# First attention layer of a two-layer kernel: mixes together behind the scores, a score bank for two of eight turns, layer norm's last step on GpSimd

## The reference, cut to what matters

```python
x = x + L0(_gn(x), ...)      # x: 1 x 128 rows x 256 tokens x 256 channels
x = x + L1(_gn(x), ...)      # _gn: group norm over all rows and tokens, 32 groups

def L0(x1d, x2d, ...):       # 8 heads of 32
    x = layernorm(x1d) * norm_w + norm_b
    q, k, v = split(x @ qkv_w.T)
    gate = sigmoid(x @ gate_w.T + gate_b)
    bias = x2d @ x2d_w.T / sqrt(32)              # the same for all 128 rows
    weights = softmax(q k^T + bias, over keys)    # 256 x 256, per row and head
    return ((weights v) * gate) @ final_w.T + final_b

def L1(x, ...):              # 4 heads of 64, keys within 16 of the query
    return banded_attention(x @ w_in.T + b_in) @ w_out.T + b_out
```

## Time and profile before

| | us |
|---|---|
| median of 3 runs (lowest, highest) | 3706.16 (3704.67, 3711.67) |
| the profiled execution, and its span | 3711.91, 3710.0 |
| busy PE, DVE, ACT, POOL over the span | 3428.1, 3129.4, 2693.5, 1993.3 |
| layer 0: first and last `ln_rstd` | 218.5, 2345.7 |
| between the layers: aggregation starts | 2398.8 |
| granted TensorE clock, mean | 0.973 of full speed |

### The profile page before, as it was taken

The page is one execution under the profiler, slowest core; times in us unless marked ns, Lnnn a source line. Parts: engine busy times, 40 slices in busy tenths (PEclk is TensorE's granted clock), DMA queues, the critical chain, the costliest instruction groups (busy, mean ns, idle before and its releaser), DMA issues.

```text
span 3710.0 us, 122532 instructions
## 1 busy us (share of the span) xinstructions
PE 3428.1 (92%) x36747; PEld 2986.1 (80%) x36747; DVE 3129.4 (84%) x11359; ACT 2693.5 (73%) x8871; POOL 1993.3 (54%) x3723
## 2 busy tenths in 40 slices
PE   4469999999999999999999999799999999999998
PEld 1157878777878787878787787599999999999998
DVE  4479999999999999999999999778888888888887
ACT  1148888888888888888888888567677667766776
POOL 0046767666666666666666666434434344444443
PEclk8579999999999999999999999899999999999999
DMA  9921111111111111111111111111111111111111
GB/s 360 354 71 46 49 46 48 48 45 50 43 51 42 51 42 51 42 51 42 51 42 51 42 51 42 41 41 51 51 56 51 51 51 57 51 51 52 55 51 47
DMA packets 189032, 238.42 MB, mean 64 GB/s; under 512 B 11824, under 2 KB 176176, under 8 KB 184752
## 3 DMA queue, kind: packets, MB, share of 16 engines
q1 hardware_dynamic: 184368, 204.17, 17.4%
q10 hardware_dynamic: 4608, 33.56, 2.5%
HBM read 170.57 MB, written 67.11 MB: 64 GB/s over the span
## 4 chain that ended last, share of the span: by engine, by line
PE 49%; DVE 16%; issue 13%; POOL 11%; ACT 5%; DMA 4%; DVEq 1%; ACTq 0%; POOLq 0%; SPq 0%
PE work L464 20%; POOL prob L359 6%; PE score L597 5%; PE work L473 5%; PE turn L504 5%; PE mix L630 4%; ACT prob L702 4%; PE score L491 3%; DMA x_chunk<-xT 3%; PE turn L614 3%; POOL g_tok L373 2%; POOL g_tok L370 2%; DVE kT L954 2%; DVE att L939 2%; DVE y_sb L890 2%
## 5 line engine op out<-in xcount | busy, mean ns | idle before, releaser
L359 POOL TENSOR_SCALAR prob<-prob,row_inv 128x256 f32<-128x256 f32 x2048 | 1049.0, 530 | 683.3 <-DVE row_inv L908 670.7
L464 PE MATMUL work<-src,w 128*128 128x256 f32 x7680 | 1074.1, 289 | 36.4 <-DVE y_sb L890 29.9
L702 ACT ACTIVATE prob<-prob,row_min 128x256 f32<-128x256 f32 x2048 | 1022.6, 504 | 39.2 <-DVE row_min L902 39.2
L464 PEld LDWEIGHTS work<-src,w 128*128 128x128 f32 x7680 | 951.9, 189 | 118.9 <-DVE y_sb L890 59.7
L902 DVE CUSTOM_DVE_ANT_0 prob<-score,neg_bias 128x256 f32<-128x256 f32 x2048 | 753.1, 419 | 111.7 <-PE score L491 100.9
L402 POOL TENSOR_SCALAR prob<-prob,row_inv 128x160 f32<-128x160 f32 x1024 | 387.9, 397 | 765.0 <-DVE row_inv L1012 765.0
L504 PE MATMUL turn<-ident,prob 128*128 128x128 f32 x4096 | 627.9, 276 | 35.2 <-DVE probT L913 29.7
L708 ACT COPY probT<-turn 128x512 f32<-128x512 f32 x512 | 299.5, 585 | 351.4 <-PE turn L504 351.4
L765 ACT ACTIVATE prob<-prob,row_min 128x160 f32<-128x160 f32 x1024 | 431.1, 426 | 136.4 <-DVE row_min L1005 136.3
L504 PEld LDWEIGHTS turn<-ident,prob 128*128 128x128 f32 x4096 | 463.9, 141 | 78.8 <-POOL prob L359 47.0
L464 PE MATMUL work<-att,wf 128*128 128x256 f32 x3072 | 429.3, 289 | 3.6 <-DVE att L939 2.2
(11 more groups left out here) (99 smaller groups left out, 5528.2 us busy)
## 6 DMA issues: line engine op xcount, KB each, us to landing
pair_chunk<-pairT ACTq DMA_DIRECT2D x32, 1024.0 KB, 7.7
x_chunk<-xT SPq DMA_DIRECT2D x32, 1024.0 KB, 8.4
x_sb<-xT SPq DMA_DIRECT2D x128, 256.0 KB, 3.4
x_tok<-x_nat SPq DMA_DIRECT2D x128, 256.0 KB, 3.3
x1T<-y_sb SPq DMA_DIRECT2D x128, 256.0 KB, 2.2
x_sb<-x1T SPq DMA_DIRECT2D x128, 256.0 KB, 2.9
outT<-y_sb SPq DMA_DIRECT2D x128, 256.0 KB, 2.2
prob<-w_d SPq DMA_DIRECT2D x1, 1024.0 KB, 8.2
```

Source lines behind the costliest of these rows:

```text
L359: pool.tensor_scalar(prob[:, h, ib], prob[:, h, ib], row_inv[:, h, ib:ib + 1], 1.0, ALU.mult, ALU.mult).then_inc(norm_done[0], 1)
L464: ins = pe.matmul(out[:, cb], w[:, of_w, kb, cols + cb * P:cols + (cb + 1) * P], x[:, of_x, kb], start=n == 0, stop=n == len(terms) - 1)
L702: act.activation(prob[:, h, ib], prob[:, h, ib], ACT.Exp, bias=row_min[:, h, ib:ib + 1], scale=-1.0, accum_out=row_sum[:, h, ib:ib + 1]).t ...
```

## The change

Seven things change in layer 0. (1) `mixes(last, 0)` and `mixes(last, 1)` stand together behind `scores(m, 1)`; before, half 0 stood in the row's own body. (2) Heads 3 and 7 are transposed into the first score bank, not into `turn`; VectorE copies them from there, and each half's scores wait for the copy. (3) The banks of the projections are dealt anew: q, k and gate in bank 0; transposed `xn`, v and y in bank 1. (4) GpSimd computes `xn` as g * rstd + off, with off = -mean * rstd from a small product of its own, one row further ahead. (5) ScalarE, not VectorE, copies the rounded part of `src`. (6) The residual leaves `final_b` out and is one addition over 512 columns, at the start of a later body; `final_b` enters layer 1's statistics as an offset and its output through `y_bias`. (7) The output statistics are taken for two rows at once, so half as many are aggregated. The order of the bodies changes on every engine. Layer 1's loop keeps its order.

```diff
 # GpSimd, body0: ahead = m + 3
+                if far.exists:
+                    wait(pool, ln_var_done, far.times(2, 2))
+                    apart(pool, pool_passed)
+                    pool.tensor_tensor(ln_rstd[:], ln_var[:], minus_half[:], ALU.pow).then_inc(ln_rstd_done, 1)
+                    wait(pool, ln_rstd_done, far.times(2, 1))
+                    pool.tensor_tensor(ln_off[:], ln_neg[:], ln_rstd[:], ALU.mult).then_inc(ln_rstd_done, 1)
+                    wait(pool, ln_rstd_done, far.times(2, 2))
+                    wait(pool, t2_done, far.times(1, 0))
+                    apart(pool, pool_passed)
+                    for tb in range(TB):
+                        pool.tensor_scalar(xn[:, tb], g_tok[:, far.base % 2, tb], ln_rstd[:, tb:tb + 1],
+                                           ln_off[:, tb:tb + 1], ALU.mult, ALU.add).then_inc(xn_done, 1)
...
 # TensorE, body0
                 def scores(r, hg):
...
+                    wait(pe, turn_done[0][1], r.times(PAIRS0, 2 * hg - 2))
...
                 def turns(h):
                     wait(pe, norm_done[0], m.times(TB * H0, TB * (h + 1)))
-
-                    if h % 2 == 0:
+                    to = turn[:]
+                    if h % HPG == HPG - 1:
+
+                        to = score[:, 0].rearrange("p b t -> p (b t)")
+                        if h < HPG:
+                            wait(pe, min_done[0], m.times(TB * H0, TB * (HPG + 1)))
+                        elif nxt.exists:
+                            wait(pe, min_done[0], nxt.times(TB * H0, TB))
+                    elif h % HPG == 0:
+                        wait(pe, turn_done[0][0], m.times(PAIRS0, h // 2))
+                    elif h % HPG == 1:
+                        wait(pe, turn_done[0][0], m.times(PAIRS0, h // 2 + 1))
+                    else:
                         wait(pe, turn_done[0][1], m.times(PAIRS0, h // 2))
...
+                if nxt.exists:
+                    wait(pe, src_done[0], nxt.times(1, 1))
+                    wait(pe, gate_done, m.times(HG, HG))
+                    project(work[:, 0], w0, 0, x).then_inc(q_ps[0], 1)
                 if m.exists:
                     scores(m, 1)
+                if last.exists:
+                    mixes(last, 0)
+                    mixes(last, 1)
+                if m.exists:
                     turns(0)
...
                 if m.exists:
                     turns(2)
-                if nxt.exists:
-                    wait(pe, q_done[0], nxt.times(1, 1))
-                    project_tokens(work[:, 0], w0, 2 * CH, x).then_inc(v_ps[0], 1)
-                if m.exists:
                     turns(3)
                 if nxt.exists:
+                    if far.exists:
+                        wait(pe, xnT_done, far.times(CB, CB))
+                    else:
+                        wait(pe, y_done[0], m.times(1, -1))
+                    project_tokens(work[:, 1], w0, 2 * CH, x).then_inc(v_ps[0], 1)
                     scores(nxt, 0)
                 if m.exists:
                     turns(4)
+                if nxt.exists:
+                    wait(pe, k_done[0], nxt.times(1, 1))
+                    project(work[:, 0], w0, 3 * CH, x).then_inc(gate_ps, 1)
+                if m.exists:
+                    turns(5)
...
 # ScalarE, body0
+                    wait(act, xnT_done, far.times(CB, CB))
+                    wait(act, gate_ps, far.times(1, -1))
+                    act.copy(src[:, far.base % 2, HIGH], xnT[:]).then_inc(src_high[0], 1)
...
 # VectorE, body0 (done = m - 2)
+                    dve.tensor_tensor(y_sb[:, :, done.base % 2], work[:, 1], x_sb[:, done.base % XSLOTS], ALU.add
+                                      ).then_inc(y_done[0], 1)
...
-                if far.exists:
-                    wait(dve, ln_rstd_done, far.times(1, 1))
-                    wait(dve, t2_done, far.times(1, 0))
-                    for tb in range(TB):
-                        dve.tensor_scalar(xn[:, tb], g_tok[:, far.base % 2, tb], ln_mv[:, tb, 0:1],
-                                          ln_rstd[:, tb:tb + 1], ALU.subtract, ALU.mult).then_inc(xn_done, 1)
...
+                    dve.tensor_scalar(ln_neg[:], ln_mv[:, :, 0], -1.0, None, ALU.mult).then_inc(ln_var_done, 1)
                     dve.tensor_scalar(ln_var[:], ln_mv[:, :, 1], EPS, None, ALU.add).then_inc(ln_var_done, 1)
...
+                if done.exists and done.base % 2 == 1:
+                    wait(dve, y_done[0], done.times(1, 1))
+                    apart(dve, dve_passed)
                     for ob in range(CB):
...
+                        dve.bn_stats(gstat1[:, ob, at], y_sb[:, ob].rearrange("p r t -> p (r t)")).then_inc(y_stats, 1)
```

More of the change, by code:

```diff
@@ L351, in body0, with norms @@
             def body0(m):
-                nxt, far = m + 1, m + 2
-                def norms(r, g):
-                    wait(pool, inv_done[0], r.times(PAIRS0, g + 1))
+                nxt, far, ahead = m + 1, m + 2, m + 3
+                g = g_tok[:, ahead.base % 2]
+                def norms(r, j):
+                    wait(pool, inv_done[0], r.times(PAIRS0, j + 1))
                     apart(pool, pool_passed)
-                    for h in (2 * g, 2 * g + 1):
+                    for h in (2 * j, 2 * j + 1):
                         for ib in range(TB):
@@ L716, in body0 @@
                     act.copy(nqT[:, nxt.base % 2, HIGH], work[:, 0]).then_inc(q_high[0], 1)
+                if m.exists:
+                    exps(m, 3)
+                    exps(m, 4)
+                    turn_copy(0)
+                if far.exists:
+                    wait(act, t2_done, far.times(1, 1))
+                    wait(act, src_done[0], far.times(1, 0))
+                    for cb in range(CB):
+                        act.activation(xnT[:, cb], work[:, 1, cb], ACT.Identity,
+                                       scale=vec0_sb[:, 0, cb:cb + 1], bias=vec0_sb[:, 1, cb:cb + 1]
+                                       ).then_inc(xnT_done, 1)
+                    wait(act, xnT_done, far.times(CB, CB))
+                    wait(act, gate_ps, far.times(1, -1))
+                    act.copy(src[:, far.base % 2, HIGH], xnT[:]).then_inc(src_high[0], 1)
+                if m.exists:
+                    exps(m, 5)
+                if nxt.exists:
+                    wait(act, k_ps[0], nxt.times(1, 1))
+                    act.copy(kT[:, nxt.base % 2, HIGH], work[:, 0]).then_inc(k_high[0], 1)
+                if m.exists:
+                    turn_copy(2)
                 if last.exists:
@@ L747, in body0 @@
                 if nxt.exists:
-                    exps(nxt, 3)
-                    wait(act, gate_ps, nxt.times(1, 1))
-                    wait(act, att_sum_done, nxt.times(1, -1))
-                    for hg in range(HG):
-                        act.activation(gate[:, nxt.base % 2, hg], work[:, 1, hg], ACT.Tanh, scale=0.5,
-                                       bias=half_gate_b[:, hg:hg + 1]).then_inc(gate_done, 1)
+                    exps(nxt, 2)
             over_rows(act, 2, 1, body0)
@@ L880, in split @@
                                   ).then_inc(src_done[n], 1)
-            def residual(n, last, bank, bias):
-                wait(dve, y_ps[n], last.times(1, 1))
-                wait(dve, y_out[n][last.base % 2], last.times(16, 0, of=2))
-                if n == 0:
-                    wait(dve, x_in[n][last.base % XSLOTS], last.times(16, 16, of=XSLOTS))
-                    apart(dve, dve_passed)
-                for ob in range(CB):
-                    dve.scalar_tensor_tensor(out=y_sb[:, last.base % 2, ob], in0=work[:, bank, ob], scalar=bias[:, ob:ob + 1],
-                                             in1=x_sb[:, last.base % XSLOTS, ob], op0=ALU.add, op1=ALU.add
-                                             ).then_inc(y_done[n], 1)
             def body0(m):
-                last, nxt, far = m + -1, m + 1, m + 2
+                last, nxt, far, ahead = m + -1, m + 1, m + 2, m + 3
                 def mins(r, h):
@@ L940, in body0 @@
                                       ).then_inc(att_done[0], 1)
-                if far.exists:
-                    wait(dve, g_done[0], far.times(1, 1))
+                if nxt.exists:
+                    mins(nxt, 0)
+                if m.exists:
+                    inverse(m, 3)
+                if nxt.exists:
+                    mins(nxt, 1)
+                    mins(nxt, 2)
+                if m.exists:
+                    turn_copy(5, turn[:])
+                if nxt.exists:
+                    mins(nxt, 3)
@@ L1026, in body1 @@
                 if (last + -1).exists:
-                    residual(1, last + -1, 1, vec1_sb[:, 2])
+                    done = last + -1
+                    wait(dve, y_ps[1], done.times(1, 1))
+                    wait(dve, y_out[1][done.base % 2], done.times(16, 0, of=2))
+                    for ob in range(CB):
+                        dve.scalar_tensor_tensor(out=y_sb[:, ob, done.base % 2], in0=work[:, 1, ob],
```

(2 more changed lines are left out.)

238 lines of the change are left out of this document (107 added, 131 removed).

## The result

| | before | after |
|---|---|---|
| median of 4 runs each, same chip (lowest, highest) | 3708.90 (3704.67, 3711.67) | 3661.44 us (3654.74, 3664.15) |
| ratio, 95% interval | | 0.987, 0.9852 to 0.9888 |
| profiled execution, span | 3711.91, 3710.0 | 3664.15, 3662.3 |
| layer 0's row, from the power step | 16.75 | (2292.4 - 223.4) / 127 = 16.29 |

What follows compares the result with a forecast made beforehand. PE's own work was the floor: 15.32 of layer 0's 16.75 us row. Waits of 0.58 and 0.02 made 15.92, plus 0.05 and 0.08, 16.05: 89 us less, seams -1, so 3616 us; range 3560 to 3725, the forecast's own 3590 to 3648.

Steps and rivals of the forecast that it cites:

- The wait ahead of head 1: On PE, head 1's turn awaits head 0's copy out of the one `turn` bank: 0.58 us in every row.
- The two paths: Through PE's order and through ScalarE's and VectorE's copies, the next row's scores were to be reached within 0.02 us.
- the mixes' lead-in: PE's delay before mixes behind scores, taken as 0.17 us; other values would shift the row by -0.17 to +0.09.
- there the layout leaves no slack, and I add 0.05: Every second row, VectorE's double statistics precede the residual, q's remainder and head 4's minima: 0.05 us added.
- rival C: Slower: delays in the loop through ScalarE to the next scores are paid in full; 17.05 us a row, 3743 us; chance 0.19.
- ScalarE's copy of head 0 starts at s+3.65: Start of ScalarE's string to the next scores, 3.65 us after `scores(m, 1)` starts on PE (s); 2.99 to k's rounded part.
- I count nothing: Token-layout input load, issued behind the residual's store on SP and needed by GpSimd half a row later: no cost.
- the caution of 0.08: 0.08 us a row added because the handovers read from the trace were the shortest kind, with idle engines.
- The port lock: VectorE's remainders of `src` and `att` could each lose 0.53 us beside GpSimd, up to 16.35 a row; not added.
- A: PE's floor alone sets the row, copies coming sooner: 15.3 to 15.7 us a row, 3523 us for 15.32; chance 0.10.
- B: Handovers on ScalarE and VectorE take longer: 16.3 to 16.7 us a row, 3673 us at 16.5; chance 0.23.
- D: GpSimd becomes late for turns, with `xn` ahead of the norms: 3700 us at most; within the no-change chance of 0.06.

Runs made afterwards that it cites:

- e1: Changed kernel with the two-row output statistics moved on VectorE to behind the copy of head 1; 3579.85 us, ratio 0.9646 to the kernel before.
- e3: Changed kernel with both edits, e1's moved statistics and e2's early load; 3576.56 us, ratio 0.9632 to the kernel before.
- e2: Changed kernel with SP issuing the load of `x_tok` first in its body, not last; 3638.37 us, ratio 0.98 to the kernel before.
- e6: e3 with the rounded copy of `src` made by VectorE again, not ScalarE; 3660.05 us, ratio 0.9864 to the kernel before.
- e5: e3 with the k projection ahead of head 1's turn, heads ordered 0, 1, 3, 2, ScalarE and VectorE rearranged; 3621.02 us, ratio 0.976.
- e10: e3 with `xn` computed by VectorE again, between the minima of heads 5 and 6; 3655.49 us, ratio 0.9864 to the kernel before.
- e9: e3 with new small tensors allocated last and the statistics tensor at its old size, so old tensors keep their SBUF addresses; 3570.81 us, ratio 0.9634.
- e4: Changed kernel with the first half's mixes back behind head 5's turn; 3725.67 us, ratio 1.0046 to the kernel before.

## Why the prediction was right, and half of it missing

**Right in direction and in the steps of the short row.** Behind the scores at s, head 0's turn stands at s+2.78 (laid out 2.95), head 1's at 4.18 (4.35) after a turn-to-turn time of 1.40 as in the earlier trace rows, the next scores at 8.55 (8.76), and from there the row ends after 7.08 (7.16). The wait ahead of head 1 is 0.55 (0.58), released by ScalarE's copy. The two paths to those scores meet as laid out: the copy of head 3 ends the wait, by less than 0.1 (from the start of v to the scores it is 1.69 in this row and 1.61 in the long row behind it, where no wait is named). All of the 0.17 that the first step is early is the mixes' lead-in, which behind scores is nothing; the prediction had named nothing as the lower end of this term. The short row is 15.63 where 15.92 was laid out, and e1 and e3, where most rows are of this kind, run at 15.73 and 15.66. The residual's wait is gone. The aggregation takes 3.64 for both blocks (7.10 in the earlier trace rows):

```profile
2348.65 3.64 DVE L880 BATCH_NORM_AGGREGATE ch_mv<-gstat 128x2 f32<-128x384 f32 x2
```

**The step that failed: "there the layout leaves no slack, and I add 0.05".** The double statistics were seen ahead of the residual, q's remainder and head 4's minima, whose exponentials stand ahead of head 0's copy, and rival C's text named this start of the loop. But they were priced by a guess. With an average of 16.29 and a short row of 15.63 the long row is 16.95, that is 1.32 more (1.5 between 800 and 2000 us), 0.66 a row on average. Part of it is the load's (next paragraph). The statistics are 1.27 of work at a place that nothing covers, and they are worth 0.56 to 0.6 a row, not 0.05: e1 gives 0.56 back by moving them alone, and in e2, without the load's part, a long row is 1.2 over a short one. The error had a simple form. The layout started ScalarE's string with "ScalarE's copy of head 0 starts at s+3.65" and never asked what must be done on VectorE before it. Counted from VectorE's copy of head 7 at s-0.82, those steps are all there in the timeline above.

**The load, "I count nothing".** It cost 0.11 a row (after to e2). SP issues it behind a store that waits for the residual, and in some long rows that is late enough to delay GpSimd's multiplication and with it the product ahead of head 4.

**Two errors of opposite sign.** The forecast was 16.05 a row, the result 16.29, 0.24 more. The statistics and the load cost 0.66 where 0.05 stood, 0.61 too little; the short row came out 0.29 under its layout, and the caution of 0.08 was not needed: 0.61 - 0.29 - 0.08 = 0.24. The number is thus nearer than its parts, which is luck. The row of 16.29 is just inside the forecast's own 15.85 to 16.3; layer 1 and the setup (below) take the time out of 3590 to 3648, and it lies in the stated range because the rivals had widened it.

**Terms with a wrong size and no effect.** In the groups by line, 800 to 2000 us:

```profile
L377 POOL TENSOR_SCALAR xn<-g_tok,ln_rstd,ln_off 128x256 f32<-128x256 f32 x147 | 80.3, 553 | 19.7 <-POOL ln_off L372 19.7
...
L915 DVE TENSOR_TENSOR src<-xnT,src 128x512 fp32r<-128x512 f32 x73 | 54.6, 748 | 0.0
...
L746 ACT CAST src<-xnT 128x512 fp32r<-128x512 f32 x74 | 46.1, 623 | 3.7
...
L372 POOL TENSOR_TENSOR ln_off<-ln_neg,ln_rstd 128x2 f32<-128x2 f32 x73 | 14.4, 197 | 5.7
```

The small product takes 0.20, not 0.7. `xn` takes 0.55 on GpSimd, where 0.53 was taken, and the copy of `src` 0.62 on ScalarE. The port lock was priced for VectorE, and by a sum that does not come out: two losses of 0.53 less half a microsecond of slack are 0.56, which is 16.6 a row and not 16.35. In the kernel after VectorE's remainder of `src` is faster than before (0.70 in the middle case and 0.75 on average, against 0.85 in the earlier trace rows), and GpSimd loses: its four products for heads 4 and 5 take 2.83 beside these remainders, and most other groups of four 1.85. So either side can pay, GpSimd 1.0 a row here and in e3, VectorE about 1.1 in e6.

```profile
1525.43 2.83 POOL L364 TENSOR_SCALAR prob<-prob,row_inv 128x256 f32<-128x256 f32 x4
...
1525.80 0.68 DVE L915 TENSOR_TENSOR src<-xnT,src 128x512 fp32r<-128x512 f32 x1
...
1526.40 0.68 DVE L981 TENSOR_TENSOR att<-att_sum,att 128x512 fp32r<-128x512 f32 x1
```

**Where the 47.8 us between the two profiled executions are.** Loop of layer 0: -58.2. From the last power step to the aggregation +3.1 (53.1 before, 56.2 after; the step stands further ahead of its row now). Aggregation and the way to layer 1: -3.0, of which the aggregation is 3.5. These two were to be -1 together and are +0.1. Layer 1: +5.5, from the addresses, not foreseen. Before the first power step: +4.9; the ten kernels of the experiments start between 212.0 and 220.6 with almost the same setup, the kernel before at 218.5 and the kernel after, the latest of all, at 223.4, so I take it for scatter of the setup; no run shows its cause.

**The rivals.** A was priced for PE's floor of 15.3 and fell for the kernel after. e3 lies in its span (15.3 to 15.7), but not by its mechanism, since the wait ahead of head 1 is there in every row; PE's own work is less than was laid out, 15.0 (15.63 less 0.55 and 0.08). B's number (3673) is nearer to the result than the forecast, though not by its reason: no handover was longer. C's mechanism was the right one for every second row, at 1.2 for the statistics, and absent in the others. D did not happen in the kernel after except in one row of four, by 0.57 on average; it did in e5 and e6.

## What to carry to other kernels

When an order is laid out on paper, start each engine's string at what it must have done before, not at the first instruction of interest: an uncovered 1.27 us every second row took 81 of the 128 us that the same kernel gains in e1, and moving it behind a later copy gave them back. An instruction that comes every second row needs its own row in the layout, since an average hides it. On engines that are busy 14 of 16 us the size of a move does not tell its price: 0.41 moved to VectorE cost 0.67 a row (e6) and 0.73 cost 0.64 (e10), each through a wait that the layout did not have.

## What the runs showed of the hardware that was not expected

The same instructions of layer 1 run 0.05 us a row slower when tensors lie at other SBUF addresses. It is the v projection alone; its matmuls in 2600 to 3400 us, in the kernel after and in e9 (the kernel before has the 130.0 and 285 of e9):

```profile
L486 PE MATMUL work<-w,src 128*128 128x256 f32 x960 | 135.0, 289 | 0.0
```

```profile
L486 PE MATMUL work<-w,src 128*128 128x256 f32 x960 | 130.0, 285 | 0.0
```

Twelve a row at 5 us / 960 = 5.2 ns more are 0.06 us, which covers the difference; the other projections are alike in both. Which of the moved tensors does it was not tried. Mixes right behind scores need no lead-in, where mixes behind transposes of 128 need 0.17 (e4's rows).
